# Masked scores that stay in PSUM for the exponential in the last attention stage of a graph network, with new order tables

## The reference, cut to what matters

```
for l in range(L):                                   # L = 2
    q = (x @ Wq[l] + bq[l]).reshape(N, H, D)         # N = 625, H = 8, D = 64
    k = (x @ Wk[l] + bk[l]).reshape(N, H, D)
    v = (x @ Wv[l] + bv[l]).reshape(N, H, D)
    a = (q[dst] * k[src]).sum(-1) * scale
    ...
    e = jnp.exp(a - amax[dst])
    denom = jax.ops.segment_sum(e, dst, num_segments=N)
    alpha = e / (denom[dst] + 1e-16)
    agg = jax.ops.segment_sum(alpha[:, :, None] * v[src], dst, num_segments=N).reshape(N, C)
    x = agg + (x @ Ws[l] + bs[l]) + enc
x = layer_norm(x, ln_g, ln_b)
x = jax.nn.relu(x @ W1 + b1) @ W2 + b2 + x
x = layer_norm(x, ln_g, ln_b)
return x + enc
```

## Time and profile before

| what | value |
|---|---|
| median of 3 runs | 1182.97 us (1182.5 to 1183.24) |
| profiled execution | 1185.03 us, of which the span from first to last instruction is 1183.2 us |
| PE busy | 1083.8 us (92%) |
| PE weight load busy | 995.4 us (84%) |
| DVE busy | 809.2 us (68%) |
| POOL busy | 710.6 us (60%) |
| ACT busy | 548.9 us (46%) |
| mean granted clock of TensorE | 0.972 of full speed |

### The profile page before, as it was taken

One profiled execution on the slowest core, in us unless ns is written; L12 is line 12 of the kernel. 1 busy time (PEld: TensorE's weight loads), 2 busy tenths in 40 slices (PEclk: granted clock), 3 DMA queues, 4 the chain that ended last, 5 costly groups with the idle time before them and its releaser, 6 DMA issues.

```text
span 1183.2 us, 20938 instructions
## 1 busy us (share of the span) xinstructions
PE 1083.8 (92%) x6814; PEld 995.4 (84%) x6814; DVE 809.2 (68%) x1562; ACT 548.9 (46%) x970; POOL 710.6 (60%) x960
## 2 busy tenths in 40 slices
PE   6889879859999999999999999999999989998697
PEld 6778777739998899988998889988899979998595
DVE  6898778565666756658567566775788767778524
ACT  7777734223552135422453225613567646666130
POOL 3553581373647755577555776569666875578662
PEclk9999989769999999999999999999999999999799
DMA  5000001231101212021120220221201101021001
...
DMA packets 39358, 56.99 MB, mean 48 GB/s; under 512 B 13829, under 2 KB 14079, under 8 KB 38877
## 3 DMA queue, kind: packets, MB, share of 16 engines
...
## 4 chain that ended last, share of the span: by engine, by line
PE 65%; DVE 4%; POOL 4%; issue 2%; ACT 1%; POOLq 0%; DVEq 0%; ACTq 0%
PE ps L312 39%; PE ps L1610 8%; PE ps L334 7%; PE ps L1904 3%; PE ps L1923 3%; PE ps L2086 2%; PE ps L1870 1%; PE ps L1584 1%; POOL w_lo L352 1%; POOL prob L431 1%; ACT prob L408 1%; DVE prob L401 1%; POOL res L1291 0%; DVE acc L1809 0%; DVE acc L1807 0%
## 5 line engine op out<-in xcount | busy, mean ns | idle before, releaser
L352 POOL TENSOR_TENSOR w_lo<-w_raw,w_hi 128x512 fp32r<-128x512 f32 x152 | 202.8, 1334 | 12.7
L312 PE MATMUL ps<-yt_hi,w_hi 128*128 128x314 f32 x640 | 201.3, 314 | 4.0 <-DVE yt_lo L1988 3.8
L312 PE MATMUL ps<-yt_hi,w_lo 128*128 128x314 f32 x640 | 197.3, 308 | 0.0
L312 PE MATMUL ps<-yt_lo,w_hi 128*128 128x314 f32 x640 | 197.0, 308 | 0.0
L431 POOL TENSOR_SCALAR prob<-prob,rinv 125x628 f32<-125x628 f32 x160 | 126.9, 795 | 105.9 <-DVE rinv L416 87.0
L375 ACT ACTIVATE pt_hi<-ps 125x625 fp32r<-125x625 f32 x160 | 109.3, 694 | 103.2 <-PE ps L334 102.0
L349 POOL TENSOR_SCALAR w_hi<-w_raw 128x512 fp32r<-128x512 f32 x152 | 96.2, 633 | 71.1 <-DMA w_raw<-L_gnn_wo 38.4
L668 PE MATMUL ps<-oh_s,oh_d 125*125 125x314 bf16 x800 | 117.3, 303 | 23.5 <-DVE oh_s L564 17.7
L668 PEld LDWEIGHTS ps<-oh_s,oh_d 125*125 125x125 bf16 x800 | 105.8, 138 | 34.6 <-DVE oh_s L564 22.9
L312 PEld LDWEIGHTS ps<-yt_hi,w_hi 128*128 128x128 f32 x640 | 121.4, 190 | 6.5 <-issue 3.5
L312 PEld LDWEIGHTS ps<-yt_hi,w_lo 128*128 128x128 f32 x640 | 121.4, 190 | 0.0
...
## 6 DMA issues: line engine op xcount, KB each, us to landing
...
```

The lines of the kernel that those rows point to most:

```text
L312: ins = pe.matmul(out_ap, lhs(i, kk), rhs(j, kk), start=kk == 0 and n == 0, stop=kk == count - 1 and n == 2)
L352: pool.tensor_tensor(w[slot][1][:, kk, 0:cols], w_raw[slot][:, kk, 0:cols], w[slot][0][:, kk, 0:cols].bitcast(FP32), ALU.subtract).then_in ...
```

## The change

DVE now writes the masked scores back into the slot from which it read them and counts a new semaphore, `t_masked`. ACT waits for that count, reads the masked scores in the slot, writes the exponential to `prob` and drains the slot. So a slot that holds a score is held through the turn of DVE and that of ACT. POOL waits for the slot to be drained where it waited for a count of exponentials. The four order tables are new; the units, the instructions of each unit and the weights are the same in number. The middle stage has code of its own for its scores and is not touched.

```
-        dve.tensor_tensor_reduce(out=halves(prob[:, u % RING_P, :]), in0=wide(s, 0, R),
+        dve.tensor_tensor_reduce(out=wide(s, 0, R), in0=wide(s, 0, R),
                                  in1=halves(mask[:, u % TILES, :]), scale=-scale, scalar=1e20, op0=ALU.add,
-                                 op1=ALU.min, accum_out=low[:, o:o + 1]).then_inc(jobs.drained[s], 1)
+                                 op1=ALU.min, accum_out=low[:, o:o + 1]).then_inc(s_masked, 1)

-    def act_exp(act, jobs, u, it, exp_done):
-        jobs.wait_drained(act, f"s{u // TILES}_{u % TILES}", it)
+    def act_exp(act, jobs, u, masked):
+        act.wait_ge(s_masked, masked)
+        s = jobs.at[f"s{u // TILES}_{u % TILES}"][0]
         o = u % SMALL_RING
-        act.activation(prob[:, u % RING_P, :], prob[:, u % RING_P, :], ACT.Exp, bias=low[:, o:o + 1], scale=-1.0,
-                       accum_out=denom[:, o:o + 1]).then_inc(exp_done, 1)
+        own(act)
+        act.activation(halves(prob[:, u % RING_P, :]), wide(s, 0, R), ACT.Exp, bias=low[:, o:o + 1], scale=-1.0,
+                       accum_out=denom[:, o:o + 1]).then_inc(jobs.drained[s], 1)

-        pool.wait_ge(ready, u + 1)
+        ready.wait_drained(pool, f"s{u // TILES}_{u % TILES}")

 LAYER_PE, first line of each:
-q0.0 q0.1 k0.0 k0.1 q1.0 s0_0 s0_1 q1.1 s0_2 - s0_3 t0_0 k1.0 s0_4 t0_1 s1_0 - k1.1 s1_1 t0_2 s1_2 - w0.0 w0.1
+q0.0 q0.1 k0.0 k0.1 q1.0 q1.1 s0_0 s0_1 s0_2 s0_3 t0_0 s0_4 t0_1 s1_0 s1_1 w0.0 t0_2 s1_2 w0.1 t0_3 - t0_4
```

More of the change, by code:

```diff
@@ L160 @@
+t4_3 t4_4 s5_3 s5_4 pv4.0 t5_0 s6_0 pv4.1 t5_1 - t5_2 s6_1 - s6_2 t5_3 s6_3 t5_4 pv5.0 s6_4 pv5.1 t6_0 s7_0
+t6_1 t6_2 s7_1 t6_3 s7_2 s7_3 t6_4 s7_4 pv6.0 t7_0 pv6.1 t7_1 t7_2 t7_3 t7_4 pv7.0 pv7.1 v0.0 v2.0 v4.0 v0.1
+v3.0 v1.0 v1.1 v2.1 v3.1 v4.1
 """.split()
 LAYER_DVE = """
-lo:q0e lo:q0o lo:k0e sc:s0_0 lo:k0o sc:s0_1 sc:s0_2 sc:s0_3 lo:q1e lo:q1o lo:t0_0 sc:s0_4 lo:t0_1 sc:s1_0
-sc:s1_1 sc:s1_2 lo:t0_2 lo:k1e lo:k1o acw:0 lo:t0_3 lo:t0_4 sc:s1_3 sc:s1_4 acp:0 lo:t1_0 sc:s2_0 lo:t1_1
-sc:s2_1 sc:s2_2 lo:t1_2 sc:s2_3 lo:t1_3 lo:t1_4 lo:q2e lo:q2o acp:1 lo:t2_0 lo:t2_1 sc:s2_4 sc:s3_0 lo:k2e
```

56 lines of the change are left out of this document (28 added, 28 removed).

## The result

| | before | after |
|---|---|---|
| median | 1183.11 us (1182.5 to 1184.26, 4 runs) | 1191.7 us (1189.77 to 1193.82, 4 runs) |
| profiled execution | 1185.03 us, span 1183.2 | 1189.77 us, span 1188.0 |
| mean granted clock in it | 0.972 | 0.974 |
| first layer, start to v jobs | 121.5 us | 124.8 us |
| second layer, start to final stage | 121.2 us | 124.4 us |

The ratio of the times is 1.0072, 95% interval [1.0053, 1.0091]: slower, and above the range that I gave. In the two profiles the layers give +3.4 and +3.2 us, the final stage +0.1; the code ahead, which the change does not touch, ended 1.8 us earlier this time. Together that is, but for rounding, the 4.8 us between the spans. The medians are 8.6 us apart, and part of that is luck of the draw: the kernel before ran four times here, between 1182.5 and 1184.3 us, and in the 109 later runs between 1182.6 and 1191.4.

The account below looks back on a forecast made before the run. POOL was taken to set each layer's end. Two layers at 0.6 - 0.04 us, less 0.8 in the final stage, gave +0.3 on 1182.97: 1183.3 us; range 1179.6 to 1187.4, with 50% on 1181.5 to 1185.3.

Parts of the forecast that it names:

- The exponential: ACT's exponential, now read from PSUM: 780 ns instead of 816, passed on only as -0.04 us a layer.
- The masking itself: DVE's masking, now written to PSUM: 0 change from 810 ns, bounds 21 ns less to 200 more; 50 dearer means wrong.
- The idle time before s0_3: Start of a layer: PE idles about 2.5 us before s0_3, behind DVE's queue.
- PE's loss up to pv0.0: Start of a layer: PE has lost 4.1 us when pv0.0 begins, against 1.6 before; under 3 or over 5 means wrong.
- No long wait for a slot between heads 1 and 4: Layer's middle: the new PE table asks no slot back too soon, so 2.7 us of PE's losses go.
- The splits behind the layers: Two k splits moved behind POOL's last scaling are done in time and cost nothing, in layers or final stage.
- six transposes moved ahead: Final stage: six transposes go ahead of pv7's drain, so n0.1 and all that follows come 0.8 us earlier, once.
- the tail: Layer's end: set by POOL, each sum ready from s4_1 on; last scaling at 117.6 us against 117.0, +0.6 a layer.
- POOL's units of 1.91 us: Layer's end: POOL needs 1.91 us a unit, counted as 19 units of 1.905 behind s4_1.
- s4_1: Score filled at 71.5 us into the layer, its sum ready for POOL 2.1 us later, at 73.6.
- slots short in the tail: Rival, 30%: slot waits at the layer's end come in series with POOL, 1.8 us a layer, giving 1186.9 us.
- The other rival: POOL's relief counts, 20%: PE loses less than 4.1 us at the start, layers end 2 us earlier, 1179.3 us.

Follow-up runs that it names:

- hold_only: Changed kernel, but masked scores go to SBUF and the exponential reads them there, as before; the slot is still released by the exponential: 1190.28 us, ratio 1.0032 to before.
- exp_first: Changed kernel with the exponential of s5_4 moved ahead of the copy of t5_0 in ACT's order: 1187.7 us, ratio 1.0014 to before.
- tables_exp_filled: Kernel before with the new tables, s5_4's exponential moved ahead, and matmuls of s0_2 and transposes of t7_2, t7_3 repeated: 1187.75 us, ratio 1.0008.
- xl_short: Changed kernel with DVE's four yt_lo passes in the first layer cut to 80 of 628 columns: 1186.02 us, ratio 1.0007 to before.
- again: The changed kernel run once more, unaltered: 1193.51 us, ratio 1.0046 to before.
- mended: Changed kernel with s5_4's exponential moved ahead, POOL's split spq0 one place earlier and s0_2's matmuls done five times: 1187.55 us, ratio 1.001 to before.

## Why the prediction was wrong

*Right.* The exponential (780, measured 784). The masking itself, 12 ns dearer, inside the bounds (but the read of its row result, which I had not priced, is 54 ns longer: together 66, more than the 50 that I named as a sign of being wrong. ACT gets a score that much later and gives back 32 in the exponential; hold_only, with both as before, has the same waits within 0.04 us). The idle time before s0_3 (2.5 us), t0_1 at 17.2, w0.0 at 19.7, PE's loss up to pv0.0 (4.2). No long wait for a slot between heads 1 and 4. The splits behind the layers cost nothing. In the final stage six transposes moved ahead, and the transposes of the normalised rows (L2072) stand 1109.73 - 1105.21 = 4.5 us behind the released ones; before it was 1105.62 - 1100.44 = 5.2. The 0.7 us came as predicted, but the rest of the stage was 0.7 longer, so nothing was left. Why is open; the mean granted clock of the stage is 0.90 in both profiles. After, then before:

```profile
1103.23 1.15 PE L2068 MATMUL ps<-ident,acc 128*125 128x128 f32 x9
1105.21 1.03 PE L2068 MATMUL ps<-ident,acc 128*125 128x128 f32 x7 [0.84 <-DVE acc L1811]
1109.73 1.07 PE L2072 MATMUL ps<-ident,nrm 125*128 125x125 f32 x4 [3.48 <-DVE nrm L2002]
```

```profile
1105.62 1.07 PE L2070 MATMUL ps<-ident,nrm 125*128 125x125 f32 x4 [3.49 <-DVE nrm L2000]
```

*Wrong: the tail.* The failed step is "from then I find each next sum there before POOL wants it, by 0.4 us at the closest". It took the handing on of a score as 2.1 us, the time at the start of a layer, and did not read ACT's order at s5_4, where a copy stands ahead that waits for PE. It was 4.0 us from the end of the score there (930.4 to 934.42), and POOL waited 0.72 us for the sum. This is also how the hold of the slot came to cost 1 us in the first layer. I had listed the short slots, but not that of s5_2, which s5_4 asks back, and thought POOL covers them; POOL covers none of what delays a sum for which it waits. exp_first bears this out: with the pause gone the layers are as long as those of the tables with the old score path and the same order (tables_exp_filled).

*Wrong: POOL's units of 1.91 us.* Where one meets a DVE pass with two SBUF operands it is 0.5 to 0.6 longer; twice in the first layer, 1.1 us, which makes it the largest of the three pieces there. The earlier trace rows has the same pass at 1006 ns; I used it only as a bound for DVE. xl_short shows it.

*Wrong: s4_1* 1.0 us late at POOL, 0.7 of it small waits of PE between heads 1 and 4 (t2_3 0.2, the others under 0.12 each) that I had set to nothing, the rest a handing on 0.3 longer than the 2.1. Nor was the 88.4 that I gave for s5_4 in the kernel before right: it began at 929.90, 88.2 us into its layer, so the new order was to be level with it and came 1.6 later.

*Not in my list: the clock.* I let PE stand 2.5 us in one piece and priced only that piece. The lower level behind it cost 0.4 to 1.0 us of the layer where it came (s5_4 at 90.2 to 90.9), and that at the end of the first layer 0.4 to 1.9 (hold_only and again, first layers less 124.8 and less what s5_4 was late). The median rose by 6.3 to 8.6 us in three comparisons where the undisturbed layers rose by 3.4 and 1.9; falls like these, one to three in each profile, can be 1 to 3 us of the difference, and the rest is chance in the code ahead or stays open.

The rival "slots short in the tail", 1186.9, came nearest in its number, and in part by luck. What came true is its condition, a score that reaches POOL later than its turn, but at s5_4, a place that it did not list. Behind s5_4 PE does stand for short slots (0.78 us before t6_1, 0.38 before t6_3 and before s7_4), and POOL has no wait for ACT there at all, so those cost nothing, as I had said. And it missed the yt_lo passes and the clock. The other rival's condition, less than 4.1 us lost at the start, was not met (4.2), and mended shows that relief of POOL ahead of s5_4 gives nothing. The Trainium skill's page "PSUM — Partial Sum Buffer" with its "evacuate promptly" would have had me put the first rival ahead. By hold_only the longer hold does cost, 2.1 of the 5 us, but not once ACT's order is mended.

What stays open: why the undisturbed s5_4 is 0.8 us later with the tables alone than before (I see only small waits), why exp_first and xl_short gain about 1 us more at equal clock than their layers show, and how the clock's falls divide over the many runs that have no profile.
